# A score maximum on the whole array, stage ends without a drain, and row sums in three groups

## What is computed

```python
x = x + 0.5 * ffn(layernorm(x), w_router, w_gate, w_up, w_down)   # top 1 of 32 experts, capacity 320
x = x + attn(layernorm(x), Wq, bq, Wk, bk, Wv, bv, Wo, bo)
x = x + 0.5 * ffn(layernorm(x), ...)
...
# attn: 16 heads of 32, rotary q and k, full attention over L = 1024
scores = einsum('bqhd,bkhd->bhqk', q, k) / sqrt(32)
out = einsum('bhqk,bkhd->bqhd', softmax(scores, axis=-1), v) @ Wo.T + bo
```

## Time and profile before

| | us |
|---|---|
| median of 3 runs (lowest, highest) | 4805.33 (4804.62 to 4808.12) |
| the profiled execution | 4800.56 |
| span of its instructions | 4798.5 |
| attention: first maximum to last sum matmul | 1628.6 to 3585.2 |
| mean granted TensorE clock | 0.968 |

### The profile page before, as it was taken

One profiled execution on the slowest core, in us unless ns is written; L12 is line 12 of the kernel. 1 busy time (PEld: TensorE's weight loads), 2 busy tenths in 40 slices (PEclk: granted clock), 3 DMA queues, 4 the chain that ended last, 5 costly groups with the idle time before them and its releaser, 6 DMA issues. The chain is left out here.

```text
span 4798.5 us, 74447 instructions
## 1 busy us (share of the span) xinstructions
PE 4382.3 (91%) x26944; PEld 2855.4 (60%) x26944; DVE 3230.0 (67%) x4432; ACT 2239.4 (47%) x3619; POOL 2409.6 (50%) x1402
## 2 busy tenths in 40 slices
PE   6779999979999599999999999999976776999998
PEld 6768998868888333333333333333325665998897
DVE  6767777756667466666666666666636886777775
ACT  4533333322222166666666666666653343333332
POOL 2333443426555366666666666666654553443442
PEclk9999999989999799999999999999997887999999
DMA  4455555535555634444444444444417553555552
GB/s 144 141 190 180 191 193 175 178 123 183 174 181 166 160 76 97 97 98 98 98 98 98 100 98 99 99 99 99 99 41 196 168 153 135 194 191 176 179 189 108
DMA packets 450030, 666.74 MB, mean 139 GB/s; under 512 B 191548, under 2 KB 192848, under 8 KB 449728
## 3 DMA queue, kind: packets, MB, share of 16 engines
q1 hardware_dynamic: 419008, 596.07, 44.5%
q0 software_dynamic: 30720, 66.62, 3.7%
HBM read 502.31 MB, written 177.80 MB: 142 GB/s over the span
## 5 line engine op out<-in xcount | busy, mean ns | idle before, releaser
L1622 DVE TENSOR_REDUCE att_big<-att_mx 128x2 f32<-128x2048 f32 x512 | 1174.2, 2293 | 665.2 <-PE att_mx L1662 665.2
L1550 POOL TENSOR_TENSOR att_pairsum<-att_p,att_p 128x1024 f32<-128x1024 f32 x512 | 1202.3, 2374 | 759.8 <-PE att_zp L1706 443.7
L1568 ACT ACTIVATE att_p<-att_st 128x512 f32<-128x512 f32 x2048 | 1112.2, 595 | 579.0 <-PE att_st L1683 487.1
L1683 PE MATMUL att_st<-att_q,att_k 128*128 128x512 f32 x2048 | 879.1, 473 | 64.9 <-ACT att_p L1568 20.4
L1683 PEld LDWEIGHTS att_st<-att_q,att_k 128*128 128x128 f32 x2048 | 343.5, 187 | 809.3 <-ACT att_p L1568 492.6
L1693 PE MATMUL att_op<-att_p,att_v 128*32 128x512 f32 x4096 | 543.3, 602 | 1.0 <-ACT att_p L1568 1.0
L892 DVE TENSOR_TENSOR e_w<-e_raw,e_w 128x2048 fp32r<-128x2048 f32 x192 | 439.0, 2286 | 41.8 <-ACT e_w L887 36.5
L911 ACT ACTIVATE e_sg<-e_gp 128x320 f32<-128x320 f32 x256 | 112.0, 438 | 730.8 <-PE e_up L181 684.9
L887 ACT ACTIVATE e_w<-e_raw 128x2048 fp32r<-128x2048 f32 x192 | 367.2, 1913 | 52.6 <-DMA e_raw<-in_w_gate 48.3
L179 PE MATMUL e_gp<-e_xT,e_w 128*128 128x320 f32 x1024 | 325.4, 318 | 0.4 <-DVE e_xT L946 0.4
L181 PE MATMUL e_gp<-e_xT,e_w 128*128 128x320 f32 x1024 | 318.3, 311 | 0.0
(11 more groups left out here) (152 smaller groups left out, 8464.9 us busy)
## 6 DMA issues: line engine op xcount, KB each, us to landing
e_raw<-in_w_gate SPq DMA_DIRECT2D x64, 1024.0 KB
e_raw<-in_w_up SPq DMA_DIRECT2D x64, 1024.0 KB
e_raw<-in_w_down SPq DMA_DIRECT2D x64, 1024.0 KB
att_q<-q SPq DMA_DIRECT2D x192, 256.0 KB, 4.2
att_k<-k SPq DMA_DIRECT2D x192, 256.0 KB, 6.3
att_mq<-q SPq DMA_DIRECT2D x128, 256.0 KB, 7.9
r_x<-in_x SPq DMA_DIRECT2D x16, 1024.0 KB
x<-r_base SPq DMA_DIRECT2D x16, 1024.0 KB, 9.4
```

The source lines that it names most:

```text
L1550: nc.gpsimd.tensor_tensor(out=pairsum[h][g % 2][:, :], in0=pr[h][2 * g % RING][:, :], in1=pr[h][(2 * g + 1) % RING][:, :], op=ALU.add).the ...
L1568: nc.scalar.activation(pr[h][kt % RING][:, c * HALF:(c + 1) * HALF], st[c][:, :], ACT.Exp, scale=SCALE).then_inc(s_exp, 1)
L1622: nc.vector.tensor_reduce(out=big[b % 2][:, :, qt, 0], in_=mx[:, :, :, :].rearrange("p h c k -> p h (c k)"), axis=AX.X, op=ALU.max).then_i ...
L1683: nc.tensor.matmul(st[c][:, :], kst[b][:, h, kt * P:(kt + 1) * P], qst[b][:, h, c * HALF:(c + 1) * HALF], start=True, stop=True).then_inc( ...
```

## The change

**Stage ends.** `Space.clear` lets VectorE clear all ranges and then has one barrier that is by semaphores only; the `Block` ends without the drain of GpSimd.

**Maximum.** `mq` and `mk` and their loads go. The rough score is made of the first 96 rows of `qst` and `kst` (all three blocks), one full-width matmul for each (head, half of the keys), into three banks `mx` of 512 columns used in turn; VectorE takes four maxima of 128 x 512 a tile into `halves`, and once a pair one small maximum over the two halves (`join`).

**Scores.** Three banks `st` in turn, in place of two; scores run one further ahead, and on TensorE one score and one rough matmul alternate. The ring `pr` has 8 tiles a head.

**Sums.** GpSimd adds the sums of groups 0 and 1 into one (`join`, one addition a head), so a pair has 10 additions and 3 `totals`, all three in the next pair at kt = 0, 2, 3; `row` moves to kt = 5 and `copy_z` to kt = 3.

```diff
             if b != a + 1:
-                self.nc.all_engine_barrier(sems_to_clear=range(lo, a + 1))
+                self.nc.vector.sem_clear(range(lo, a + 1))
                 lo = b
+        self.nc.all_engine_barrier(sem_only=True)
...
-        return self.ctx.enter_context(self.nc.Block())
+        return self.ctx.enter_context(self.nc.Block(no_gpsimd_drain=True))
...
+    NB = 3
-    RING = 4
+    RING = 8
-    ROW = TURN + 1
+    ROW = TURN + 2
-    TOTALS = {KT - 2: 0, KT - 1: 1, 0: 2, 2: 3}
+    NA, NZ = 10, 3
+    ADDED = (0, 2, 6, 8)
+    JOINED = 4
+    PLACE = (0, 1, 1, 2)
+    READY = (6, 8, 10)
+    TOTALS = {0: 0, 2: 1, 3: 2}
...
-        st = S.pair(ps, "st", [P, HALF])
-        mx = ps("mx", [P, 2, 2, HALF])
+        st = [ps(f"st{n}", [P, HALF]) for n in range(NB)]
+        mx = [ps(f"mx{n}", [P, HALF]) for n in range(NB)]
...
-                for c in range(2):
-                    rows = slice(2 * c * HD, 2 * (c + 1) * HD)
-                    sp.dma_start(mq[b][rows, :].bitcast(F32), q_in[0, src[0], :]).then_inc(s_in[b], 16)
-                    sp.dma_start(mk[b][rows, :].bitcast(F32), k_in[0, src[0], half(c)]).then_inc(s_in[b], 16)
...
                 pool.wait_ge(s_exp, CH * p + 4 * (2 * g + 1) + 2 * h + 2)
-                pool.wait_ge(s_z, past(NG2 * p + g - 1))
-                nc.gpsimd.tensor_tensor(out=pairsum[h][g % 2][:, :], in0=pr[h][2 * g % RING][:, :],
+                if g < 2:
+                    pool.wait_ge(s_z, past(NZ * (p - 1) + g + 1))
+                if g == 2:
+                    pool.wait_ge(s_add, NA * p + JOINED + h + 1)
+                if g == 3:
+                    pool.wait_ge(s_z, NZ * p)
+                nc.gpsimd.tensor_tensor(out=pairsum[h][PLACE[g]][:, :], in0=pr[h][2 * g % RING][:, :],
...
+            def join(p, h):
+                pool.wait_ge(s_add, NA * p + ADDED[1] + h + 1)
+                nc.gpsimd.tensor_tensor(out=pairsum[h][0][:, :], in0=pairsum[h][0][:, :],
+                                        in1=pairsum[h][1][:, :], op=ALU.add).then_inc(s_add, 1)
...
-                nc.vector.tensor_reduce(out=big[b % 2][:, :, qt, 0], in_=mx[:, :, :, :].rearrange("p h c k -> p h (c k)"),
-                                        axis=AX.X, op=ALU.max).then_inc(s_max, 1)
+                for h in range(2):
+                    for c in range(2):
+                        n = 4 * qt + 2 * h + c
+                        dve.wait_ge(s_mx, CH * p + n + 1)
+                        nc.vector.tensor_reduce(out=halves[:, h, qt, c:c + 1], in_=mx[n % NB][:, :], axis=AX.X,
+                                                op=ALU.max).then_inc(s_max, 1)
...
-                pe.wait_ge(s_max, KT * p + qt)
-                for c in range(2):
-                    for h in range(2):
-                        rows = slice((2 * c + h) * HD, (2 * c + h + 1) * HD)
-                        last = nc.tensor.matmul(mx[:, h, c, :], mq[b][rows, qt * P:(qt + 1) * P], mk[b][rows, :],
-                                                start=True, stop=True)
-                last.then_inc(s_mx, 1)
+                pe.wait_ge(s_max, past(NM * p + prior(n) + (1 if n >= NB else 0)))
+                nc.tensor.matmul(mx[n % NB][:, :], qst[b][0:3 * HD, h, qt * P:(qt + 1) * P],
+                                 kst[b][0:3 * HD, h, half(c)], start=True, stop=True).then_inc(s_mx, 1)
...
-                pe.wait_ge(s_exp, past(CH * p + 4 * kt + x - 1))
+                pe.wait_ge(s_exp, past(CH * p + prior(4 * kt + x) + 1))
...
-                    for x in (2, 3):
-                        scores(p, b, kt, x)
-                    if kt < TURN and left:
-                        rough(*nxt, FIRST + kt)
-                    if kt >= TURN and left >= 2:
-                        rough(*ahead(i, b, 2), kt - TURN)
-                    for x in (0, 1):
-                        if kt + 1 < KT:
-                            scores(p, b, kt + 1, x)
+                    for x in range(4):
+                        if x == 0:
+                            scores(p, b, kt, 3)
+                        elif kt + 1 < KT:
+                            scores(p, b, kt + 1, x - 1)
                         elif left:
-                            scores(p + 1, nxt[1], 0, x)
+                            scores(p + 1, nxt[1], 0, x - 1)
+                        if kt < TURN and left:
+                            rough(*nxt, 4 * (FIRST + kt) + x)
+                        if kt >= TURN and left >= 2:
+                            rough(*ahead(i, b, 2), 4 * (kt - TURN) + x)
```

More of the change, by code:

```diff
@@ L1439, in attention @@
         kst = [sb(f"k{b}", [P, 2, L], F32R) for b in range(DEPTH)]
-        mq = [sb(f"mq{b}", [P, L], F32R) for b in range(DEPTH)]
-        mk = [sb(f"mk{b}", [P, HALF], F32R) for b in range(DEPTH)]
         v = [sb(f"v{b}", [P, KT, 2, HD]) for b in range(DEPTH)]
         pr = [[sb(f"p{h}_{t}", [P, L]) for t in range(RING)] for h in range(2)]
-        pairsum = [S.pair(sb, f"pairsum{h}", [P, L]) for h in range(2)]
+        pairsum = [[sb(f"pairsum{h}_{t}", [P, L]) for t in range(NZ)] for h in range(2)]
+        halves = sb("halves", [P, 2, KT, 2])
         big = S.pair(sb, "big", [P, 2, KT, HD])
@@ L1470, in attention, with prior @@
         N_OUT = 4
-        N_IN = 3 + 3 + 2 + 2 + 1
+        N_IN = 3 + 3 + 1
         def tile(h, c):
             return slice((2 * h + c) * HD, (2 * h + c + 1) * HD)
+        def prior(n):
+            return n - NB if n >= NB else max(m for m in range(CH) if m % NB == n) - CH
         def half(c):
@@ L1556, in step @@
                         add(DEPTH * i + b, g, h)
+                    if g == 1:
+                        for h in range(2):
+                            join(DEPTH * i + b, h)
             rounds_out(DEPTH, NP, step)
@@ L1599, in step @@
                             copy_o(*last)
-                        if last and (kt, x) == (2, 1):
+                        if last and (kt, x) == (3, 1):
                             copy_z(*last)
@@ L1618, in maxima, with join @@
                 p = DEPTH * i + b
-                dve.wait_ge(s_mx, KT * p + qt + 1)
                 if qt == 0:
-                    dve.wait_ge(s_row, past(p - 1))
-                nc.vector.tensor_reduce(out=big[b % 2][:, :, qt, 0], in_=mx[:, :, :, :].rearrange("p h c k -> p h (c k)"),
-                                        axis=AX.X, op=ALU.max).then_inc(s_max, 1)
+                    dve.wait_ge(s_max, NM * p)
+                for h in range(2):
+                    for c in range(2):
[3 more added lines that the diff above has]
+                                                op=ALU.max).then_inc(s_max, 1)
+            def join(i, b):
+                p = DEPTH * i + b
+                dve.wait_ge(s_max, NM * (p + 1) - 1)
+                dve.wait_ge(s_row, past(p - 1))
+                nc.vector.tensor_reduce(out=big[b % 2][:, :, :, 0], in_=halves[:, :, :, :], axis=AX.X,
+                                        op=ALU.max).then_inc(s_max, 1)
             def copy_row(i, b):
@@ L1634, in step @@
                         maxima(*ahead(i, b, 1), qt)
+                    join(*ahead(i, b, 1))
                 for qt in range(FIRST):
@@ L1642, in _ @@
                 maxima(0, 0, qt)
+            join(0, 0)
             copy_row(0, 0)
@@ L1695, in products, with totals @@
                 last.then_inc(s_v, 1)
-            def totals(p, g, left):
-                pe.wait_ge(s_add, 2 * (NG2 * p + g) + 2)
+            def totals(p, g):
+                pe.wait_ge(s_add, NA * p + READY[g])
                 if g == 0:
@@ L1702, in totals @@
                     for h in range(2):
-                        pe.wait_ge(s_rowq[h], 2 * (p + (2 if left else 1)))
+                        pe.wait_ge(s_rowq[h], 2 * min(p + 2, NP))
                 for h in range(2):
                     for c in range(2):
-                        last = nc.tensor.matmul(zp[tile(h, c), :], ones[:, :], pairsum[h][g % 2][:, half(c)],
-                                                start=g == 0, stop=g == NG2 - 1)
+                        last = nc.tensor.matmul(zp[tile(h, c), :], ones[:, :], pairsum[h][g][:, half(c)],
+                                                start=g == 0, stop=g == NZ - 1)
                 last.then_inc(s_z, 1)
@@ L1715, in step @@
                 for kt in range(KT):
-                    if kt == 2 and before:
-                        totals(p - 1, TOTALS[kt], left)
+                    if kt in (2, 3) and before:
+                        totals(p - 1, TOTALS[kt])
                     if kt == ROW and left:
@@ L1724, in step @@
                     if kt == 0 and before:
[L1725 to L1741 removed]
+                        totals(p - 1, TOTALS[kt])
+                    for x in range(4):
[3 more added lines that the diff above has]
+                            scores(p, b, kt + 1, x - 1)
+                        elif left:
+                            scores(p + 1, nxt[1], 0, x - 1)
[3 more added lines that the diff above has]
```

(10 more changed lines are left out.)

24 lines of the change are left out of this document (9 added, 15 removed).

## The result

| | before | after |
|---|---|---|
| median, us (lowest, highest; 4 runs each) | 4806.73 (4804.62 to 4815.04) | 4674.54 (4672.12 to 4677.2) |
| ratio, 95% interval | | 0.9722 (0.9705 to 0.9739) |
| the profiled execution, and its span | 4800.56, 4798.5 | 4673.33, 4671.3 |
| mean granted TensorE clock | 0.968 | 0.969 |

The change saves 132 us by the medians, 127 by the two profiled executions. The forecast was 4658 with a range of 4635 to 4724: the time is inside, 17 us above the forecast.

A forecast was written before the change was run, and what follows sets the result against it. The prediction took a TensorE, ScalarE, TensorE chain through two score banks as the bound. Savings of 106 + 4.8 + 3.7 + 3.6 + 26.9 + 2.0 = 147 us gave 4658, range 4635 to 4724.

The forecast's parts named there:

- The step of 3.06: Attention step on TensorE with three banks: 3.06 us in place of 3.19, a gain of 0.13 a step.
- The `totals` term: Sums in attention: one `totals` less on TensorE saves 0.84 us a pair, its joins going to GpSimd.
- The pair of 28.1: Steady attention: a pair of heads takes 28.1 us against 29.81, saving 106 us over 62 pairs.
- 0.2 for the stall: Once a pair `copy_row` puts VectorE late in step 5, counted as a stall of 0.2 us.
- Last two pairs, 4.8: End of attention: steps without maxima fall to about 2.28 us; 5.8 saved in pair 63, 1 lost in the last.
- Start, 3.7: Start of attention: first maxima to first score takes 38.2 us in place of 41.9, saving 3.7.
- The first load's 3.6: Start of attention: the first load shrinks from 2.5 to 1.8 MB, taken as 3.6 us saved.
- Stage ends, 26.9 + 2.0: Ends of stages: GpSimd's drains after the routing and expert stages save 26.9 us, fewer barriers in six stages 2.0.
- rival by which the drain's work comes back: Stage ends: GpSimd's next instruction waits instead of the drain, giving 4685 us; chance 0.11.
- The alternation: Rival on attention's alternating matmuls: they stall, the step returns to 3.19 or so, giving 4721 us; chance 0.16.
- case that the change makes the kernel slower: Attention: each switch between 96-row and 128-row matmuls exposes the weight load, step 3.64, giving 4931 us; chance 0.08.
- rule on packing: Four packed 32-row tiles give 3.07 times the rate; unpacking would cost some 250 us if TensorE's stream were the bound.

The follow-up runs named there:

- e3: The changed kernel with two score banks in place of three, all else as changed: 4830.82 us, ratio 1.004 to the kernel before.
- e4: The changed kernel with the three banks numbered on from pair to pair instead of restarting at each pair: 4653.28 us, ratio 0.9673.
- e5: The changed kernel without GpSimd's joins (8 additions a pair), TensorE summing four groups a pair: 4722.54 us, ratio 0.9817.
- e1_ends: The kernel before with only the new stage ends (no GpSimd drain, one barrier by semaphores, clears on VectorE): 4783.59 us, ratio 0.9944.
- e8: The kernel before with only the Block's GpSimd drain left out, clearing barriers kept: 4810.72 us against 4809.28, ratio 1.0002.
- e2_attention: The changed kernel with the old stage ends (drain and clearing barriers as before): 4699.51 us, ratio 0.977.
- second profile of before: The unchanged kernel before, run and profiled once more: 4806.41 us, its second routing stage (r2) 449.7 where the first profile showed 443.6.

## Why the prediction came out as it did

**What bounded the kernel: right.** The chain score, exponential, bank free, score was the bound. e3 brings it back and loses the whole gain. The steps without maxima, which the prediction named as its proof, went from 3.19 to 2.61, though the chain still sets them.

**The step of 3.06: right to a hundredth.** 3.05 in the timeline, 3.07 in the median. So 8 x 3.06 + 3 x 0.86 + 0.87 = 27.93 is the pair, and e4's 27.99 is that. The `totals` term (0.84; a step shows 0.86) is confirmed by e5.

**The pair of 28.1, 106 us: mis-sized.** It is 28.31, and 61 steady distances by 1.51 are 92, so 14 less. The term that failed is the last one, "0.2 for the stall" of `copy_row`: that stall doesn't appear (e4 has `copy_row` as well and leaves 0.06 over). In its place stands one at kt = 7 from the restart of the bank numbers, 0.31 in the timeline, 0.32 a pair by e4. That it is near 0.2 is luck. It makes 0.12 of the 0.24 by which the pair is longer than the sum of 28.07; the rest is a hundredth in each step and two in each `totals`. The prediction held three banks to mean three matmuls of distance everywhere; the diff's `prior` has the exception written out.

**Last two pairs, 4.8: 7.1, by two errors against each other.** The two last distances between output copies are 26.09 and 23.03 against 29.8 and 28.48, 9.2 saved, and 2.1 are given back behind the last step. A step without maxima is 2.61, not 2.28: the prediction let the products follow the exponential of the step's first score, but the fourth score has to wait for that exponential first (2.27 by its own sum, then 0.33 to the products: 2.60). So pair 63 saves 3.7 where 5.8 was counted. The last pair was to lose 1 and saves 3.3: GpSimd does hold up its end, as forecast, but its ten additions begin 2.4 us after the start of the pair's first step, where 7.7 was counted.

**Start, 3.7: it is 7.1.** The step "52 x 0.72" failed: queued maxima start 0.60 apart, not 0.72. That is shorter than the duration of one, and a trace shows it only where they are queued. The prediction had the like in its hands for ScalarE, whose exponentials last 0.60 and follow each other at 0.49. The first load's 3.6 measured 3.8 (stage start to first rough matmul 15.1, then 11.3).

**Stage ends, 26.9 + 2.0: size near, reason incomplete.** e1_ends gave 27.6, the stage table gives 21 (both inside 7 us of each other's error). What the text treated as two independent edits, the drain with 26.9 and the barriers with 2.0, is one: the drain alone gives nothing (e8). The rival by which the drain's work comes back to GpSimd's next instruction falls, since it comes 8.2 us earlier. Stage r1 saved 3.9 of the 5.6 counted. It takes 248.4 to 251.0 in the seven kernels with the new ends, where 246.7 was to be expected, and with the old ones 251.8 in e8 and 254.3 in e2_attention. Why, stays open.

**The rivals.** The alternation doesn't stall (0.234 and 0.238 between starts). The 96-row matmul costs what a 128-row one costs, so the case that the change makes the kernel slower falls at its first term. The rule on packing, named in the prediction, is held off by the chain that was the bound, as said there: the four serial maxima take 4 x 0.23 of the new step. Now that TensorE's stream is the bound, packed maxima would be worth their price again; with three score banks they would need nine banks in all, and this wasn't tried.

**The total.** Steady pairs 92 for 106, ends of attention 7.1 for 4.8, first pair 1.9 that wasn't counted, start 7.1 for 3.7, load 3.8 for 3.6, stage ends 21 for 28.9: 133 for 147, by the stage table against the second profile of before, and 132 by the medians. Some 22 us were counted too much and 8 too little, so the total is nearer than its terms. The prediction's time was taken against a first profile whose r2 was some 6 us short.

## What to carry to other kernels

When an engine waits for a buffer that another must empty, work out the whole loop before costing its parts; a third buffer and an order that puts other work between two uses of it were worth more here than any operation saved. Rotate buffers by a number that runs on through the loop, or make the count in a loop a multiple of the buffers. A wait moves to the next instruction of its kind unless all of them go, so try an edit in its parts before crediting one of them. An operation moved to an engine with idle time is not free if it stands in front of something that the bounding engine waits for.

## What the hardware showed unexpectedly

- A drain of GpSimd behind indirect DMAs that have all landed takes 5.3 us in the routing stages and 8.1 in the expert stages, at whichever drain comes first, and a barrier by semaphores alone doesn't pay it.
- Queued maxima of 128 x 512 from PSUM last 0.68 each and start 0.60 apart.
- An addition on VectorE with both inputs in SBUF, begun while one of GpSimd runs, ends 1.08 after GpSimd's, whenever it began, and the waiting is inside its recorded duration.
- The same program had its TensorE clock fall 20 us later in one execution than in another, and its stage was about 6 us shorter.
